# A 768-wide expert layer whose products and transposes all take 64 rows in one half of the array

## What is computed

```python
for g in range(G):                      # G = 4 groups of E = 8 experts, M = 768
    h = jax.nn.gelu(jnp.einsum('nd,edm->enm', xf, W1[g]) + b1[g][:, None, :], approximate=False)
    o = jnp.einsum('enm,emd->end', h, W2[g]) + b2[g][:, None, :]
    y = y + jnp.einsum('end,ne->nd', o, combine[:, g, :])
```

## Time and profile before

| | us |
|---|---|
| median of 3 runs (785.11 to 786.42) | 786.02 |
| span of the profiled execution | 782.1 |
| outside the span, by the median | 3.9 |
| TensorE matmuls busy | 672.5 |
| VectorE / ScalarE / GpSimd busy | 426.2 / 236.5 / 323.5 |
| granted TensorE clock, mean of the span | 0.899 |

### The profile page before, as it was taken

How to read it: one execution, slowest core, us unless ns; L and a number is a source line. 1 busy time by engine, 2 the same in 40 slices (tenths; PEclk the granted TensorE clock), 3 DMA queues, 4 the chain that set the end, 5 groups by cost and what they waited for, 6 DMA issues and landing times.

```text
span 782.1 us, 19902 instructions
## 1 busy us (share of the span) xinstructions
PE 672.5 (86%) x6348; PEld 571.2 (73%) x6348; DVE 426.2 (55%) x1247; ACT 236.5 (30%) x673; POOL 323.5 (41%) x265
## 2 busy tenths in 40 slices
PE   5957858898989996863379899999999999999995
PEld 5724646656745885753269789999999999999994
DVE  7574583745479559977934344444444434434342
ACT  3112312123247211111433333333343333333331
POOL 4730730011023322520334456555564655655554
PEclk9976968577999998975579999999999999999998
DMA  9900000000000030013116765464545665565432
GB/s 349 255 2 3 3 3 2 3 1 3 1 1 1 1 122 1 1 68 132 30 31 164 217 170 116 119 182 81 164 113 161 172 169 161 115 163 114 103 50 38
DMA packets 34982, 70.05 MB, mean 90 GB/s; under 512 B 6353, under 2 KB 21234, under 8 KB 34930
## 3 DMA queue, kind: packets, MB, share of 16 engines
q0 software_dynamic: 15840, 17.71, 13.5%
q10 hardware_dynamic: 8064, 33.12, 12.6%
q1 hardware_dynamic: 11026, 18.48, 7.3%
HBM read 59.31 MB, written 9.98 MB: 89 GB/s over the span
## 4 chain that ended last, share of the span: by engine, by line
PE 62%; DVE 17%; DMA 6%; issue 4%; POOL 1%; ACTq 1%; ACT 1%; DVEq 0%; POOLq 0%
PE bank L1492 17%; PE bank L1484 12%; PE bank L1487 7%; PE bank L1340 4%; PE bank L1469 3%; PE bank L1272 3%; PE bank L1292 3%; DMA arena<-normed_rows,fetch_u 3%; PE bank L1356 2%; DMA out_dram<-arena,number_u 2%; PE bank L1310 1%; PE bank L1283 1%; DVE zx L894 1%; DVE arena L1097 1%; DVE arena L1094 1%
## 5 line engine op out<-in xcount | busy, mean ns | idle before, releaser
L631 POOL DMA_INDIRECT out_dram<-arena,number_u x80 | 127.0, 1587 | 51.6 <-DMA out_dram<-arena,number_u 26.3
L625 POOL DMA_INDIRECT arena<-normed_rows,fetch_u x80 | 78.3, 979 | 114.9 <-DMA out_dram<-arena,number_u 51.0
L1179 DVE COPY arena<-bank 128x256 f32<-128x256 f32 x81 | 34.4, 425 | 119.5 <-PE bank L1469 110.8
L796 ACT ACTIVATE arena<-bank,arena 128x128 f32<-128x128 f32 x234 | 64.5, 375 | 115.5 <-PE bank L1487 115.5
L1492 PE MATMUL bank<-arena 128*128 128x192 f32 x468 | 83.0, 326 | 0.1
L1492 PEld LDWEIGHTS bank<-arena 128*128 128x128 f32 x468 | 75.4, 190 | 0.5 <-ACT arena L796 0.5
L1197 DVE TENSOR_SCALAR arena<-bank,arena 128x192 f32 x80 | 33.4, 418 | 59.1 <-PE bank L1492 57.5
L533 POOL TENSOR_SCALAR rstd<-mv 128x4 f32<-128x4 f32 x12 | 2.7, 229 | 147.5 <-DVE mv L883 147.5
L1484 PE MATMUL bank<-arena 128*128 128x128 f32 x468 | 59.1, 276 | 1.4 <-DVE arena L1179 1.1
L1484 PEld LDWEIGHTS bank<-arena 128*128 128x128 f32 x468 | 56.9, 192 | 3.0 <-issue 1.5
L796 ACT ACTIVATE arena<-bank,w_space 128x128 f32<-128x128 f32 x132 | 36.5, 375 | 67.0 <-PE bank L1487 67.0
(11 more groups left out here) (241 smaller groups left out, 1263.8 us busy)
## 6 DMA issues: line engine op xcount, KB each, us to landing
arena<-in_moe_w_dram ACTq DMA_DIRECT2D x14, 579.0 KB, 6.1
arena<-in_moe_w_dram ACTq DMA_DIRECT2D x14, 576.0 KB, 4.2
arena<-in_xf_dram SPq DMA_DIRECT2D x8, 512.0 KB, 9.8
w_space<-in_moe_w_dram ACTq DMA_DIRECT2D x7, 579.0 KB, 5.8
w2small<-in_moe_w_dram ACTq DMA_DIRECT2D x7, 579.0 KB, 5.6
w_space<-in_moe_w_dram ACTq DMA_DIRECT2D x7, 576.0 KB, 4.2
wab<-in_moe_w_dram ACTq DMA_DIRECT2D x7, 576.0 KB, 4.3
arena<-in_w_dram SPq DMA_DIRECT2D x8, 480.0 KB, 9.1
```

Source lines behind the costliest of these rows:

```text
L625: pool.indirect_dma_start(out=mo_stage[:, s * ROWN:(s + 1) * ROWN], out_offset=None, in_=normed_rows, in_offset=bass.IndirectOffsetOnAxis( ...
L631: pool.indirect_dma_start(out=out, out_offset=bass.IndirectOffsetOnAxis(ap=number_u[:, s:s + 1], axis=0), in_=mo_res[:, s * D:(s + 1) * D] ...
L796: nc.scalar.activation(mo_hT[:, m, :], bank[2 + m][:, 0:P], ACT.Gelu, bias=b1[:, m:m + 1]).then_inc(free[2 + m], 1)
L1179: nc.vector.tensor_copy(mo_xT.rearrange("p k t -> p (k t)"), bank[1][:, 0:2 * P]).then_inc(free[1], 1)
```

## The change

All products of the expert layer now take 64 rows. The first layer's 192 rows are three chunks c = 0, 1, 2 of 64; chunk 0 lies in the lower half of the array, chunk 1 in the upper, and chunk 2, which is held in both halves, in the lower for even and in the upper for odd blocks m. The 18 products stand in nine slots, one in either half each (`LOWER`, `UPPER`). In one slot the halves write different banks. A bank that one half has begun is then taken over by the other: the three products of either half in slots 1, 2 and 3 raise `lower_handed` or `upper_handed`, and those in slots 4, 5 and 7 wait for it.

The second layer's sums are split: the lower half sums in bank 0, the upper in bank 1. VectorE multiplies the first by the gate and adds the second times the gate. The four transposes of 64 by 128 go to banks 2 and 3, after the second layer's products have read two of the six hidden blocks. Their columns are copied out by two copies of 128 elements in place of one of 256.

```diff
@@ constants
+LOWER = ((0, 0), (0, 2), (3, 0), (5, 0), (1, 0), (2, 0), (2, 2), (4, 0), (4, 2))
+UPPER = ((1, 1), (1, 2), (2, 1), (4, 1), (0, 1), (3, 1), (3, 2), (5, 1), (5, 2))
+HANDED, TAKEN = (1, 2, 3), {4: 1, 5: 2, 7: 3}
@@ take_columns(i), on VectorE
-                dve.wait_ge(full[1], i + (moe_base[1] + 1))
-                nc.vector.tensor_copy(mo_xT.rearrange("p k t -> p (k t)"), bank[1][:, 0:2 * P]).then_inc(free[1], 1)
+                dve.wait_ge(sem("columns_lower"), i + 1)
+                nc.vector.tensor_copy(mo_xT[:, :, 0:REST], bank[2][:, 0:P].rearrange("p (k t) -> p k t", k=2)).then_inc(sem("columns_taken"), 1)
+                dve.wait_ge(sem("columns_upper"), i + 1)
+                nc.vector.tensor_copy(mo_xT[:, :, REST:P], bank[3][:, 0:P].rearrange("p (k t) -> p k t", k=2)).then_inc(sem("columns_taken"), 1)
@@ the loop of VectorE, behind the product with the gate
+                    dve.wait_ge(full[1], rest)
+                    dve.sem_inc(sem("scaling"), 1)
+                    dve.wait_ge(free[0], summing)
+                    stt(out=mo_new[:, bass.ds(new, D)], in0=bank[1][:, 0:D], scalar=mo_gates[:, bass.ds(gate, 1)], in1=mo_new[:, bass.ds(new, D)],
+                        op0=ALU.mult, op1=ALU.add).then_inc(free[1], 1)
@@ transpose_rows(i), on TensorE
+                lower, upper = slice(0, REST), slice(REST, P)
                 for k in range(2):
-                    ins = nc.tensor.transpose(bank[1][:, k * P:(k + 1) * P], mo_x[:, k * P:(k + 1) * P], ident[:])
-                ins.then_inc(full[1], 1)
+                    a_ = nc.tensor.transpose(bank[2][:, k * REST:(k + 1) * REST], mo_x[lower, k * P:(k + 1) * P], ident[lower, lower])
+                    b_ = nc.tensor.transpose(bank[3][:, k * REST:(k + 1) * REST], mo_x[upper, k * P:(k + 1) * P], ident[upper, upper])
+                a_.then_inc(sem("columns_lower"), 1)
+                b_.then_inc(sem("columns_upper"), 1)
@@ the loop of TensorE
+                    pe.wait_ge(sem("columns_taken"), i * 2 + 2)
+                    for slot in range(len(LOWER)):
+                        for half in range(2):
+                            m, c = (LOWER, UPPER)[half][slot]
+                            r, k, at_ = half * REST, c // 2, HID + m // 2 * P if c == 2 else m * P
+                            if slot in TAKEN:
+                                pe.wait_ge(sem(("upper_handed", "lower_handed")[half]), i * 3 + TAKEN[slot])
+                            ins = mm(bank[2 + m][:, 0:P], w1e[r:r + REST, at_:at_ + P], mo_xT[r:r + REST, k, :],
...
                     pe.wait_ge(free[0], i + moe_base[0])
+                    pe.wait_ge(free[1], i + moe_base[1])
                     for m in range(MC):
                         pe.wait_ge(free[2 + m], i + (moe_base[2 + m] + 1))
-                        ins = mm(bank[0][:, 0:D], mo_hT[:, m, :], w2e[:, m, :], start=(m == 0), stop=(m == MC - 1))
-                    ins.then_inc(full[0], 1)
+                        for half in range(2):
+                            r = half * REST
+                            ins = mm(bank[half][:, 0:D], mo_hT[r:r + REST, m, :], w2halves[half][:, m, :], start=(m == 0), stop=(m == MC - 1))
+                            if m == MC - 1:
+                                ins.then_inc(full[half], 1)
+                        if m == 1:
+                            transpose_rows(i + 1)
```

More of the change, by code:

```diff
@@ L788, in expert @@
                     act.wait_ge(full[0], first + moe_base[0])
+                    act.wait_ge(full[1], first + moe_base[1])
                     load_expert(act, (u + AHEAD - 1) % AHEAD, e + AHEAD - 1)
@@ L793, in expert @@
                     act.wait_ge(full[0], i + moe_base[0])
+                    act.wait_ge(full[1], i + moe_base[1])
                     for m in range(MC):
@@ L1171, in stage_rows @@
                 dve.wait_ge(sem("rows_in"), i * 16 + 16)
-                dve.wait_ge(full[1], i + moe_base[1])
+                dve.wait_ge(sem("columns_lower"), i + 0)
+                dve.wait_ge(sem("columns_upper"), i + 0)
                 nc.vector.tensor_copy(mo_gates[:, bass.ds(i % 4 * NE, NE)], mo_stage[:, bass.ds(i % STAGE * ROWN + D, NE)])
@@ L1192, in _ @@
                     new = dve.snap(i % 4 * D)
-                    added, summing = dve.snap(i + 1), dve.snap(i + (moe_base[0] + 1))
+                    added, summing, rest = dve.snap(i + 1), dve.snap(i + (moe_base[0] + 1)), dve.snap(i + (moe_base[1] + 1))
                     half, tile, ahead = dve.snap(i % 2), dve.snap(i + 0), dve.snap(i + 4)
@@ L1201, in _ @@
                     nc.vector.tensor_copy(number_u[:, bass.ds(half, 1)], table_u[:, bass.ds(tile, 1)])
-                    dve.wait_ge(free[0], summing)
+                    dve.wait_ge(free[1], rest)
                     nc.vector.tensor_copy(mo_res[:, bass.ds(to, D)], mo_new[:, bass.ds(new, D)]).then_inc(sem("result_ready"), 1)
@@ L1480, in expert @@
                 pe.wait_ge(sem(f"in_expert{u}"), 32 * (e // AHEAD + 1))
+                w2halves = [w2e[0:REST], w2e[REST:P]]
                 with pe.Fori(first, end) as i:
-                    pe.wait_ge(free[1], i + (moe_base[1] + 1))
-                    for m in range(MC):
-                        mm(bank[2 + m][:, 0:P], w1e[:, m * P:(m + 1) * P], mo_xT[:, 0, :], start=True, stop=False)
-                    for m in range(MC):
-                        r, c = m % 2 * REST, HID + m // 2 * P
-                        mm(bank[2 + m][:, 0:P], w1e[r:r + REST, c:c + P], mo_xT[r:r + REST, 1, :], start=False, stop=True).then_inc(full[2 + m], 1)
@@ L1488, in expert @@
-                    transpose_rows(i + 1)
+                    pe.wait_ge(sem("columns_taken"), i * 2 + 2)
[6 more added lines that the diff above has]
+                            ins = mm(bank[2 + m][:, 0:P], w1e[r:r + REST, at_:at_ + P], mo_xT[r:r + REST, k, :],
+                                     start=((m, c) in ((0, 0), (3, 0), (5, 0), (1, 1), (2, 1), (4, 1))), stop=((m, c) in ((0, 1), (1, 0), (2, 2), (3, 2), (4, 2), (5, 2))))
+                            if slot in HANDED:
+                                ins.then_inc(sem(("lower_handed", "upper_handed")[half]), 1)
+                            elif (m, c) in ((0, 1), (1, 0), (2, 2), (3, 2), (4, 2), (5, 2)):
+                                ins.then_inc(full[2 + m], 1)
@@ L1489, in expert @@
                     pe.wait_ge(free[0], i + moe_base[0])
+                    pe.wait_ge(free[1], i + moe_base[1])
                     for m in range(MC):
                         pe.wait_ge(free[2 + m], i + (moe_base[2 + m] + 1))
-                        ins = mm(bank[0][:, 0:D], mo_hT[:, m, :], w2e[:, m, :], start=(m == 0), stop=(m == MC - 1))
-                    ins.then_inc(full[0], 1)
-            for m in range(MC):
-                pe.wait_ge(free[2 + m], moe_base[2 + m])
+                        for half in range(2):
[5 more added lines that the diff above has]
+                            transpose_rows(i + 1)
```

4 lines of the change are left out of this document (3 added, 1 removed).

## The result

The changed kernel takes 818.62 us (median of 4 runs, 816.15 to 824.39), the one before 785.57 beside it: a ratio of 1.044, interval 1.039 to 1.049. The forecast was 772.5, the range ended at 789.

A forecast was written before the change was run, and what follows sets the result against it. TensorE was taken to bound the kernel, busy 313.1 of 315 us. From 786.0 us, −24.0 − 1 − 2 + 6.0 + 2.5 + 5 = −13.5 gave 772.5 us, with a range from 759 to 789.

The forecast's parts named there:

- TensorE's steps: TensorE's tile: 2.01 first layer, 1.95 second, 0.22 transposes; 4.18 us against 4.53, saving 24.0 us on 68.5 tiles.
- the 0.22 that I took: TensorE's four transposes: two pair steps of 0.11 us, 0.22 together, bounds 0.11 and 0.33.
- VectorE's work: VectorE: the added operation 0.41 us, 0.45 with its wait; two column copies of 0.28 each, 0.52 with overlap.
- the 4.42 of the forecast: An expert's first tile: VectorE's late column copies make it take in effect 4.42 us, against 4.18.
- +0.24: Lateness of VectorE's column copies at each of 25 experts' first tiles: +0.24 us each, +6.0 in all.
- The sum without the transfers: Terms without GpSimd's: TensorE −24.0, first tiles −1, L1484's waits −2, experts' starts +6.0, gelus behind weight loads +2.5 us.
- Hand-over at 0: First layer on TensorE: six added waits for handed-over banks cost 0, since 0.17 us remain for the semaphore.
- my bound of +8: First layer's hand-over: if a wait shows, some 0.05 to 0.1 us a tile, up to +8 us.
- Within a plain tile both are hidden: VectorE in tiles other than an expert's first: the added operation and two column copies cost no time.
- GpSimd's +5 (0 to +30): GpSimd and its DMAs: late scatters stall VectorE and the column copies; +5 us, bounds 0 and +30.
- Lateness that feeds itself: Rival: after weight loads GpSimd can't catch up before the next expert, and half of 69 tiles take 5.1; 799 us, chance 0.09.
- Added increments are held up: Rival on TensorE: each added increment holds a product up to a step of 0.11; 0 to 70 us, chance 0.03.

The follow-up runs named there:

- e1: The changed kernel without the indirect transfers of the expert loop (no gather from the fifth tile on, no scatter): 749.7 us.
- b1: The kernel before without the indirect transfers of the expert loop, the same edit as e1: 771.6 us.
- f1: The kernel before with the first layer in nine slots of 64-row pairs, each block's products in one half, so no hand-over: 800.4 us.
- e4: The kernel before with only the changed first layer (nine slots, with hand-over); transposes, second layer and VectorE's work as before: 812.5 us.
- f2: The kernel before with six more increments a tile, one on each full-height first-layer product, that nobody waits for: 786.0 us.
- r6: The changed kernel with the four transposes one block earlier, behind the second layer's first pair of blocks: 810.1 us.
- r5: The changed kernel with the four transposes directly behind the first layer, ahead of the second: 813.0 us.
- e2: The changed kernel without the scatters of the expert loop, gathers kept: 763.7 us.
- e3: The changed kernel without the gathers of the expert loop, scatters kept: 764.2 us.
- v8: The kernel before with GpSimd's scatter ahead of its gather in each tile: 805.8 us.
- f5: The kernel before with each of the first layer's six full-height products cut into two of 64 columns: 882.2 us.

## Why the prediction was wrong

- **TensorE's steps: right.** 64-row products with 192 columns pair: in e1 the pairs start 0.163 us apart, as I had it, and those of the first layer 0.112 (0.1115). The transposes were mis-sized: pairs start 0.055 apart (568.32, 568.38), so 0.11 together, half of the 0.22 that I took and my lower bound. Against that the second layer takes 2.02 us in e1 (0.66 from 566.39 to 567.05, 1.36 from 567.17 to 568.53), not 1.95. The two nearly cancel, which is luck. Plain tiles of e1 take 4.13 to 4.25 us (45 of 47), forecast 4.18, and those of b1 4.53.
- **VectorE's work: right.** 418 ns for the added operation (0.41), 291 and 279 for the copies (0.28). In e1, tiles in which VectorE reads its registers take 4.34 to 4.41 us (25 of 32, the others more, mostly at the start): the 4.42 of the forecast, and its +0.24.
- **The sum without the transfers: right.** My terms but GpSimd's give −24.0 − 1 − 2 + 6.0 + 2.5 = −18.5 us; 79 tiles of e1 against b1 give −18.9, the medians −22.
- **Hand-over at 0: wrong beside the transfers.** In e1 the first layer's weight loads wait for a product once, for 0.3 us. With the transfers the hand-over's increments are held as well, and TensorE itself waits, 8.0 us in 13 places; my bound of +8 was for a wait in every tile, not for this. f1, without the hand-over, is 12 us faster than e4 by the medians, but their intervals overlap.
- **"Within a plain tile both are hidden", and with it GpSimd's +5 (0 to +30): the step that failed.** The transfers' cost rises from 14 us (b1 to before) to 69 (e1 to changed), by 55, where I had 5. And it doesn't come the way I priced it, by a GpSimd that can't keep up. Then its waits for VectorE would fall from 37 us to a few, as I wrote; they rose to 72 (62.8, and 9.0 for L1216), so in the main it is GpSimd that is kept waiting. TensorE's increments come late while it works. I took 0 for the way from a transpose to VectorE and held the columns' copies to be hidden in a plain tile; that is true only while an increment arrives when the matmul ends. Of the transposes' increments half came 1.3 us late or more, and from 455 us on TensorE stood still for the copies for 28.3 us. My list of what would prove the forecast wrong had it, "if the columns' copies are late in plain tiles", with no mechanism behind.
- **The rivals.** "Lateness that feeds itself" (799, 0.09) named the right engine and sign, but a wrong cause, so its sign was right by luck. "Added increments are held up" had the right word. It was priced by the step of a product, and there f2 shows 0: six more increments take 786.0 us, within 0.6% of before. By the Trainium skill ("TensorE: Matmul & The Clock Gate", section "The cost: per-tile semaphore tail", 26.3 ns an increment) six of them would be an estimated 12.6 us over 80 tiles if each were exposed; the trace shows them out of the way of the products: from the first product to L1487 it is 1.43 us in f2 as before. What cost here was the 0.5 to 2.2 us after which an increment arrives, a thing the rows of before could not show, as not one of 635 was held.
- **Moving the transposes behind the second block** left 1.1 us between them and the tile's end in place of 1.8. I costed this room against VectorE's work only. How much of the loss it carries was not settled: r6 and r5, with 0.33 and 0.6 us more of it, got 9 and 6 of 33 us back, neither clear of noise; they lost most of the wait for the columns, but r5 has a longer tile of its own. And e4, where the transposes stand where they stood before, loses 27.

**What stays open:** why an increment is held. Shown is that it needs an indirect transfer of GpSimd, that in e2 and e3 it is over before the transfer's packets move, that more passes or more increments each bring it on, and that the order of the transfers matters (v8). Which resource is used up, and whether matmul passes draw on it or only come with something that does, the runs don't tell.

## What to carry to other kernels

A semaphore from TensorE was not always there when its matmul had ended. Where GpSimd issues indirect transfers beside a dense stream of matmuls, ask of every hand-over from TensorE to another engine how much room it has. f2's copies have 1.4 us and its holds cost nothing, the changed kernel's have 0.6; that more room alone mends the loss no run here showed. Look for it first in a profile as a copy that starts long after the matmul it waits for, near the end of an indirect transfer. To learn what an edit of one engine is worth, take the suspected partner out of both kernels, before and after: the pair e1 and b1 settled what the sum could not. And read in each variant the tile that the suspect left alone, or its own cost is taken for an answer, as first with r5 and e5.

## What the runs showed of the hardware

- TensorE's increments were held by up to 2.2 us during GpSimd's indirect transfers of 128 rows (0.98 us a gather, 1.59 us a scatter), 60% of those due in or within 0.4 us after one in the changed kernel, none of 1260 outside in e1. ScalarE's increments, and those of TensorE's sequencer, were not. VectorE's increments (520, the latest 0.012 us after its end) were not either. The matmuls themselves went on at their pace (pairs 0.112 and 0.163 us apart in the changed kernel as in e1).
- The hold came with GpSimd's instruction and not with the transfer's packets: in e2, with gathers alone, held increments went out 0.37 to 0.56 us after its end, and the packets moved from some 0.6 us after it. Plain weight loads at 99 GB/s held none (e1).
- Four 64-row transposes of 64 columns take 0.11 us in pairs (0.055 a pair), while a full-height pass of 64 columns takes 0.112 alone (f5), as much as one of 128.
- Increments that were held went out one behind the other, most of them 0.034 to 0.043 us apart.
